# The half routers of a gated-expert kernel spread over other places, with GpSimd waiting for VectorE in all of them

## The chip, the core and the metric

The kernel runs on one core of one Trainium2 chip. The metric is the device time of one execution in microseconds (us). The engines are TensorE (PE, with PEld for its weight loads), VectorE (DVE), ScalarE (ACT), GpSimd (POOL) and SyncE (SP), which issues the DMAs here.

## The reference

The input x is (16, 64, 112, 112): 16 images, 64 channels, 112 x 112 pixels. Cut to what matters:

```python
x = x + scale(_ln_c(x))          # max and mean over the channels, a 3x3 convolution, a sigmoid as a gate
t = _to_tokens(x)                # each pixel is a token of 64 channels
n = _ln_t(t)
router_probs = softmax(n @ router_w + router_b)          # 8 experts
top_p, top_i = top_k(router_probs, 2)
top_p = top_p / sum(top_p)
expert_out = einsum('bnd,edc->bnec', n, expert_w) + expert_b
t = t + einsum('bnk,bnkc->bnc', top_p, take_along_axis(expert_out, top_i))
```

For each token the router needs the largest and the second largest of 8 logits, each as a one-hot row in which only the first of tied logits counts, and two gates that are sigmoids of the gap between the two.

## The kernel before

**Rounds, steps and places.** The images are handled as 8 pairs. The program is one sequence of rounds; in round r three stages run interleaved, each for another pair: A (pair r: loading, centring by matmul, statistics), B (pair r-1: norms, convolution and router, on all pixels of the pair at once) and C (pair r-2: the expert matmuls and the output). Rounds 2 to 7 hold all three; round 0 is A alone, round 1 A and B, round 8 B and C, rounds 9 and 10 C alone. A round has 14 steps of 8 image rows, and each step has two halves on VectorE. So a round has 28 places: place 2s is the first half of step s, place 2s+1 the second.

**Stage C.** Per step TensorE spreads gates over channels into the PSUM tile gb (line 514). VectorE multiplies gb with the pixels xd into gx for six units (line 714); for two more, ScalarE copies gb to gs (line 1003) and GpSimd multiplies (line 1205). TensorE then adds up the experts (line 568) in moe, and VectorE adds moe to tt into the output tile ot (line 727). gb has two slots, so a spread matmul waits for the VectorE product that frees its slot. GpSimd also does the parts subtraction (line 1211, first half of a step) and tt (line 1222, second half).

**Stage B on VectorE** is put into places by `gate`: before the first unit of a half step, the place's operations are issued. Places 1, 2, 3 and 7, 8, 9 hold the two reciprocal roots (`root_guess`, `square_times_e` with line 799 and 801, `third_order`, `second_order`), place 6 `affine`, and place 9 ends with `scale`, which writes rho. Places 12 to 19 hold the router of the first half of the pixels, places 20 to 27 that of the second half: top (line 733, a reduction), ge (736, a comparison), key (741) and key_max (733), oh1 (749) and dl (751), top2 (733) and gap (760), ge2 (736), key2 (741) and key_max2 (733), oh2 (766). The names are the program's order lists; lines 741 and 733 serve both keys. Between key_max and oh1, and between key_max2 and oh2, ScalarE widens the key to 8 columns (`widen`, line 1046); after gap it makes the two gates (`gates`, lines 1052 and 1053). The operations of line 736, 741, 749, 751, 760, 766, 799 and those like them read two SBUF tensors; the reductions read one.

**Stage B on GpSimd** (`router` and `router_tail`): at step 0 `root_of` 1 makes e (line 1295) for the root of place 1; at step 1 `to_pool` (lines 1307, 1309, after tt) makes the convolution's input; at step 3 `affine_of_mean` and `root_of` 2, for place 7; at steps 5 to 7 the scaled and biased logits (lines 1244, 1252); at step 9 `first_gates` (1259) of half 0, at 10 `second_gates` (1265), at 11 `summed_gates` (1274), at 12 `scaled_gates` (1280), at 13 `first_gates` of half 1. `router_tail` does the other three of half 1 in steps 0, 1 and 2 of the next round, ahead of `router`.

**Order between the two engines.** `vector_place` makes GpSimd wait, before its gx of a place, until VectorE has ended that place's operations. In rounds 1 to 7 it does this in places 1, 2, 3, 6, 7, 8, 9 and 26; in round 8 also in places 12 to 27.

The convolution is in TensorE's order in step 2 (`convolve`, line 592), between the spread matmuls of place 5's half and the experts.

Of the kernel before, what the change touches and what calls it, by code (L numbers as in the profile page):

```python
# [52 lines left out]
LAG = 2  # L53
# [25 lines left out]
B_ACT = ("sig", "wide_0", "g1_0", "g2_0", "qa_0", "wide2_0", "wide_1", "g1_1", "g2_1", "wide2_1", "qa_1")  # L79
# [56 lines left out]
def gated_expert_program(nc, x, conv_w, conv_b, router_w, router_b, expert_w, expert_b, const_f, const_g, out):  # L136
# [3 lines left out]
    with ExitStack() as ctx:  # L140
# [57 lines left out]
        rho = sb("rho", [W, 2 * H])  # L198
# [48 lines left out]
        b_dve = sem("b_dve")  # L247
        b_pool = sem("b_pool")
# [48 lines left out]
        b_sem = {B_DVE: b_dve, B_NORM: b_norm, B_POOL: b_pool, B_ACT: b_act}  # L297
# [376 lines left out]
        def _(dve):  # L674
# [63 lines left out]
            def largest_key(r, h, again, rows):  # L738

                own(r, f"ge{again}_{h}")  # L740
                dve.tensor_tensor(key[:, rows, :], ge[:, rows, :], prios, ALU.mult).then_inc(b_dve, 1)
                own(r, f"key{again}_{h}")
                largest(key_max, key, rows).then_inc(b_dve, 1)

            def first_expert(r, h):

                rows = (first, second)[h]
# [6 lines left out]
            def second_logit(r, h):  # L754

                rows = (first, second)[h]
# [5 lines left out]
            def second_expert(r, h):  # L762

                rows = (first, second)[h]
# [643 lines left out]
```

## Time and profile before

| what | value |
|---|---|
| median of 3 runs | 1400.77 us (1400.72 to 1402.35) |
| the profiled execution | 1400.0 us, span of its instructions 1398.1 us |
| TensorE busy | 1291.5 us, 92% of the span |
| VectorE busy | 1243.4 us, 89% |
| GpSimd busy | 1065.5 us, 76% |
| ScalarE busy | 1051.3 us, 75% |
| mean granted TensorE clock | 0.968 |

Busy shares are averages over rounds of different kinds. The wait that ends last in a place is to be looked for in that place: who waits, and for whom. In a timeline, a bracket behind an instruction gives how long its engine had been idle and what released it. An instruction that is held after it was issued shows as a longer one.

### The profile page before, as it was taken

The page shows a single profiled execution, that of the slowest core. Times are in us where ns is not written, and L with a number is a line of the kernel's source. Part 1 is how long each engine was busy: PE and PEld are TensorE (multiplying, and loading weights), DVE is VectorE, ACT ScalarE, POOL GpSimd, SP SyncE. Part 2 cuts the span into 40 slices and gives each one's busy share as a digit, 9 for nine tenths or more (in the row PEclk, how much of TensorE's full clock was granted, in tenths as well). Part 3 has the DMA queues.
Part 4 walks back from the last instruction along what each step waited for, and adds up shares of the span by engine and source line. Part 5 has one row for each costly group of instructions (what it writes and reads, how often), then busy time and mean ns, then how long its engine had stood idle before and what let it go on. Part 6 is the DMA issues. An engine that isn't in the chain of part 4 may idle for free.

```text
span 1398.1 us, 33104 instructions
## 1 busy us (share of the span) xinstructions
PE 1291.5 (92%) x11750; PEld 610.9 (44%) x11750; DVE 1243.4 (89%) x1527; ACT 1051.3 (75%) x3950; POOL 1065.5 (76%) x643
## 2 busy tenths in 40 slices
PE   8854999999999999999999999999999898889998
PEld 8854444444444444444444444444444332223332
DVE  6787799978999899998999889998999889998887
ACT  6677898888988889888898889888988443444442
POOL 6333787887887787887878787887878777789885
PEclk9955999999999999999999999999999998999999
DMA  6442466666666666576676566676665554557774
GB/s 224 124 129 78 145 199 199 198 199 199 199 186 215 195 205 204 176 225 193 204 209 197 189 212 197 193 218 188 207 207 171 152 170 143 164 165 206 204 205 144
DMA packets 85845, 259.97 MB, mean 186 GB/s; under 512 B 13744, under 2 KB 13744, under 8 KB 85680
## 3 DMA queue, kind: packets, MB, share of 16 engines
q1 hardware_dynamic: 85680, 257.85, 61.3%
q8 instruction: 94, 1.54, 0.5%
q14 instruction: 71, 0.58, 0.1%
HBM read 206.42 MB, written 51.38 MB: 184 GB/s over the span
## 4 chain that ended last, share of the span: by engine, by line
PE 56%; DVE 22%; issue 9%; POOL 2%; ACT 2%; DVEq 0%; POOLq 0%; ACTq 0%
PE moe L568 34%; DVE gx L714 12%; PE tm L493 8%; PE gb L514 8%; PE tm L507 2%; DVE ge L736 2%; DVE stats L691 2%; PE moe L562 2%; PE tm L553 2%; DVE ot L727 1%; PE tm L592 1%; DVE oh L749 1%; DVE u L799 1%; POOL dl L1265 1%; DVE top L733 1%
## 5 line engine op out<-in xcount | busy, mean ns | idle before, releaser
L568 PE MATMUL moe<-gx,wc 128*64 128x448 f32 x3584 | 803.7, 554 | 0.0
L714 DVE TENSOR_TENSOR gx<-gb,xd 128x896 f32<-128x896 f32 x672 | 710.6, 1085 | 82.0 <-PE gb L514 76.8
L1205 POOL TENSOR_TENSOR gx<-gs,xd 128x896 f32<-128x896 f32 x224 | 491.0, 2192 | 233.8 <-ACT gs L1003 170.1
L1003 ACT ACTIVATE gs<-gb 128x896 f32<-128x896 f32 x224 | 205.3, 917 | 187.0 <-PE gb L514 181.7
L965 ACT ACTIVATE sq<-xct 112x64 f32<-112x64 f32 x1400 | 338.4, 246 | 7.5 <-DVE early_s L701 2.1
L568 PEld LDWEIGHTS moe<-gx,wc 128*64 128x64 f32 x3584 | 223.5, 136 | 212.2 <-issue 160.8
L965 ACT ACTIVATION_READ_ACCUMULATOR sq<-xct 112x1 f32 x1400 | 265.6, 190 | 0.0
L1222 POOL TENSOR_TENSOR tt<-xc,a1s 128x896 f32<-128x896 f32 x112 | 235.7, 2104 | 11.5 <-issue 9.8
L514 PE MATMUL gb<-s,cg 32*128 32x448 f16 x1792 | 166.7, 360 | 60.5 <-DVE gx L714 59.1
L514 PEld LDWEIGHTS gb<-s,cg 32*128 32x128 f16 x1792 | 45.3, 91 | 386.3 <-DVE gx L714 357.1
L493 PE MATMUL tm<-rhs,xa 64*112 64x74 f32 x2800 | 184.6, 272 | 10.9 <-ACT early_l L950 5.2
L493 PEld LDWEIGHTS tm<-rhs,xa 64*112 64x112 f32 x2800 | 161.6, 182 | 45.7 <-issue 40.3
L727 DVE TENSOR_TENSOR ot<-moe,tt 128x448 f32<-128x448 f32 x224 | 137.3, 613 | 15.5 <-PE moe L568 15.5
L946 ACT ACTIVATE xct<-tm 112x512 f32<-112x512 f32 x175 | 104.0, 594 | 58.1 <-PE tm L493 58.0
L1010 ACT ACTIVATE a1s<-tm,ones 128x896 f32<-128x896 f32 x112 | 112.7, 1007 | 30.3 <-PE tm L553 30.3
L1211 POOL TENSOR_TENSOR parts<-q,parts 112x448 f16<-112x448 f32 x112 | 116.4, 1040 | 9.4 <-ACT parts L988 9.4
L995 ACT ACTIVATE s<-tm 128x896 f16<-128x896 f16 x112 | 101.6, 907 | 0.0
L691 DVE TENSOR_REDUCE stats<-xct 112x8 f32<-112x512 f32 x128 | 86.6, 677 | 6.9 <-ACT logit_mean L950 6.7
L691 DVE TENSOR_REDUCE early_s<-xct 112x8 f32<-112x512 f32 x96 | 65.0, 678 | 19.7 <-ACT early_l L950 19.0
L562 PE MATMUL moe<-s,bw 128*64 128x448 f16 x448 | 80.8, 355 | 0.0
L507 PEld LDWEIGHTS tm<-cg,parts 112*64 112x64 f16 x1792 | 57.2, 111 | 48.1 <-issue 48.1
L988 ACT ACTIVATE parts<-q 112x576 f16<-112x576 f32 x112 | 75.9, 678 | 0.0
(94 smaller groups left out, 1094.4 us busy)
## 6 DMA issues: line engine op xcount, KB each, us to landing
xd<-in_x_dram SPq DMA_DIRECT2D x448, 224.0 KB, 4.0
xa<-in_x_dram SPq DMA_DIRECT2D x112, 448.0 KB, 4.4
xc<-in_x_dram SPq DMA_DIRECT2D x112, 448.0 KB, 4.8
out_dram<-ot SPq DMA_DIRECT2D x112, 448.0 KB, 3.5
gx<-in_const_g_dram SPq DMA_DIRECT2D x1, 384.0 KB, 5.6
cf<-in_const_f_dram SPq DMA_DIRECT2D x1, 333.5 KB, 3.1
cf<-in_L_ffn_expert_b_dram SPq DMA_DIRECT2D x12, 1.0 KB
gx<-in_L_ffn_expert_w_dram SPq DMA_DIRECT2D x1, 128.0 KB, 5.5
```

Of the source, the lines that this page charges most:

```text
L493: last = pe.matmul(pair[:, b, j, :], xa[chans, step % XA, row * W:(row + 1) * W], rhs1[chans, :], start=True, stop=True)
L514: last = pe.matmul(gb[:, 2 * slot + b, 0:HALF], cg[rows, k * P:(k + 1) * P], s[rows, v % 2, c * HALF:(c + 1) * HALF], start=True, stop=True)
L568: last = pe.matmul(moe[b * CH:(b + 1) * CH, c, 0:HALF], wc[:, k * CH:(k + 1) * CH], gx[:, u, b, :], start=False, stop=(k == KT - 1), skip_ ...
L691: dve.tensor_reduce(to[:, 0, lo + cols.start:lo + cols.stop], xct[:, step % 2, cols, :], AX.X, ALU.max) \
L714: dve.tensor_tensor(gx[:, i, :, :], gb[:, 2 * slot:2 * slot + 2, 0:HALF], xd[:, v % 2, :, c * HALF:(c + 1) * HALF], ALU.mult).then_inc(sca ...
L727: dve.tensor_tensor(ot[:, sl, cols], moe[:, c, 0:HALF], tt[:, sl, cols], ALU.add).then_inc(final, 1)
L965: last = act.activation(sq[:, n, :], xct[:, step % 2, n, :], ACT.Square, accum_out=to[:, 1, lo + n:lo + n + 1])
L1003: act.activation(gs[:, j, :, :], gb[:, 2:4, 0:HALF], ACT.Copy).then_inc(gate_out, 1)
L1010: act.activation(a1s[:, v % 2, :].rearrange("p (c t) -> p c t", c=2), tm[:, :, 0:HALF], ACT.Identity, bias=ones[:, :], scale=1.0).then_inc ...
L1205: pool.tensor_tensor(gx[:, ND + j, :, :], gs[:, j, :, :], xd[:, v % 2, :, j * HALF:(j + 1) * HALF], ALU.mult).then_inc(scaled_p, 1)
L1211: pool.tensor_tensor(quadrants(v)[:, :, :, QN:QUAD], q_blocks(v, AGAIN, BLOCK), high_again(v), ALU.subtract).then_inc(rest1, 1)
L1222: pool.tensor_tensor(tt[:, sl, :], xc[:, sl, :], a1s[:, sl, :], ALU.mult).then_inc(scaled_x, 1)
```

## The change

The 12 operations of a half router on VectorE go into 10 places instead of 8: oh1 and dl part, key2 and key_max2 part. Half 0 takes places 12 to 21 and half 1 starts at 22. Its last three groups come in the next round: ge2 in place 0, key2 and key_max2 together in place 4, oh2 in place 5. They have a semaphore of their own, `b_late`. ScalarE's `gates` of half 0 moves from step 8 to 9, its second `widen` from 9 to 10, half 1's first `widen` from 11 to 12, its `gates` from 12 to step 0 and its second `widen` from 13 to step 2 of the next round. On GpSimd, half 0's `second_gates`, `summed_gates` and `scaled_gates` go from steps 10, 11, 12 to 11, 12, 13; half 1's `first_gates` goes from step 13 to step 0 of the next round, `second_gates` from 0 to 3, `summed_gates` and `scaled_gates` from 1 and 2 both to 4, and `router_tail` now comes after `router`. rho gets two buffers, since the late `scaled_gates` reads it while the next round's is written; `scale` waits for the round before last instead of the last one. `vector_place` waits in all router places in all rounds, the late ones too. In the diff, lines without a change are mostly left out, of the fifth part the removed lines too; a few small hunks (the b_late semaphore, rhos for rho, the group that a wait names) are not shown.

```diff
@@ -70,13 +70,14 @@
+B_LATE = ("ge2_1", "key2_1", "key_max2_1", "oh2_1")
-         + tuple(n + "_1" for n in HALF_ROUTER))
+         + tuple(n + "_1" for n in HALF_ROUTER if n + "_1" not in B_LATE))
-B_ACT = ("sig", "wide_0", "g1_0", "g2_0", "qa_0", "wide2_0", "wide_1", "g1_1", "g2_1", "wide2_1", "qa_1")
+B_ACT = ("sig", "wide_0", "qa_0", "g1_0", "g2_0", "wide2_0", "wide_1", "g1_1", "g2_1", "qa_1", "wide2_1")
@@ -313,19 +315,20 @@
-        PLACE_END = {1: "t_a1", 2: "y_a1", 3: "r1", 6: "v2", 7: "t_a2", 8: "y_a2", 9: "rho",
-                     26: "key_max2_1"}
-        TAIL_END = {1: "t_a1", 2: "y_a1", 3: "r1", 6: "v2", 7: "t_a2", 8: "y_a2", 9: "rho"}
-        HALF_END = ("top", "ge", "key_max", "dl", "d", "ge2", "key_max2", "oh2")
-        for place in range(16):
-            TAIL_END[12 + place] = f"{HALF_END[place % 8]}_{place // 8}"
+        ROOT_END = {1: "t_a1", 2: "y_a1", 3: "r1", 6: "v2", 7: "t_a2", 8: "y_a2", 9: "rho"}
+        HALF_END = {12: "top_0", 13: "ge_0", 14: "key_max_0", 15: "oh1_0", 16: "dl_0", 17: "d_0", 18: "ge2_0",
+                    19: "key2_0", 20: "key_max2_0", 21: "oh2_0", 22: "top_1", 23: "ge_1", 24: "key_max_1",
+                    25: "oh1_1", 26: "dl_1", 27: "d_1"}
+        LATE_END = {0: "ge2_1", 4: "key_max2_1", 5: "oh2_1"}
-            ends = TAIL_END if r == PAIRS else PLACE_END
-            if 1 <= r <= PAIRS and place in ends:
-                b_done(eng, r, B_DVE, ends[place])
+            if r <= PAIRS and place in ROOT_END:
+                b_done(eng, r, B_DVE, ROOT_END[place])
+            if r <= PAIRS and place in HALF_END:
+                b_done(eng, r, B_DVE, HALF_END[place])
+            if 2 <= r <= PAIRS + 1 and place in LATE_END:
+                b_done(eng, r - 1, B_LATE, LATE_END[place])
@@ -735,35 +738,53 @@
+            def tie_key(r, h, rows):
+                own(r, f"ge_{h}")
+            def first_of_ties(r, h, rows):
+                own(r, f"key_{h}")
+            def second_tie_key(r, h, rows, group):
+                b_done(dve, r, group, f"ge2_{h}")
+                dve.tensor_tensor(key[:, rows, :], ge[:, rows, :], prios, ALU.mult).then_inc(b_sem[group], 1)
+            def second_of_ties(r, h, rows, group):
+                b_done(dve, r, group, f"key2_{h}")
+                largest(key_max, key, rows).then_inc(b_sem[group], 1)
+            def first_expert(r, h, rows):
+            def logits_left(r, h, rows):
+            def second_logit(r, h, rows):
+            def second_at_top(r, h, rows, group):
+                own(r, f"top2_{h}")
+                at_top(dl, top2, rows).then_inc(b_sem[group], 1)
+            def second_expert(r, h, rows, group):
+                dve.tensor_tensor(oh2[:, rows, :], prios, ge[:, rows, :], ALU.is_equal).then_inc(b_sem[group], 1)
@@ -775,18 +796,32 @@
                 elif place == 2:
-                    largest_key(r, h, "", rows)
+                    tie_key(r, h, rows)
+                    first_of_ties(r, h, rows)
                 elif place == 3:
-                    first_expert(r, h)
+                    first_expert(r, h, rows)
                 elif place == 4:
-                    second_logit(r, h)
+                    logits_left(r, h, rows)
                 elif place == 5:
-                    own(r, f"top2_{h}")
-                    at_top(dl, top2, rows).then_inc(b_dve, 1)
+                    second_logit(r, h, rows)
                 elif place == 6:
-                    largest_key(r, h, "2", rows)
+                    second_at_top(r, h, rows, B_DVE)
+                elif place == 7:
+                    second_tie_key(r, h, rows, B_DVE)
+                elif place == 8:
+                    second_of_ties(r, h, rows, B_DVE)
                 else:
-                    second_expert(r, h)
+                    second_expert(r, h, rows, B_DVE)
+            def late_router(r, place):
+                if place == 0:
+                    second_at_top(r, 1, second, B_LATE)
+                elif place == 4:
+                    second_tie_key(r, 1, second, B_LATE)
+                    second_of_ties(r, 1, second, B_LATE)
+                elif place == 5:
+                    second_expert(r, 1, second, B_LATE)
@@ -834,9 +869,9 @@
-                if due(count := b_at(r, len(B_POOL), 0)):
+                if due(count := b_at(r - 1, len(B_POOL), 0)):
-                dve.scalar_tensor_tensor(out=rho[:, :], in0=av, scalar=1.0, in1=r2[:, :],
+                dve.scalar_tensor_tensor(out=rhos[:, r % 2, :], in0=av, scalar=1.0, in1=r2[:, :],
@@ -859,10 +894,10 @@
                     scale(r)
-                elif 12 <= place < 20:
+                elif 12 <= place < 22:
                     half_router(r, 0, place - 12)
-                elif place >= 20:
-                    half_router(r, 1, place - 20)
+                elif place >= 22:
+                    half_router(r, 1, place - 22)
...
@@ -899,6 +936,8 @@
+                    if tail:
+                        late_router(r - 1, 2 * step + 1)
                     if Bp:
...
@@ -1056,15 +1095,18 @@
                     widen(r, 0, "")
-                elif step == 8:
+                elif step == 9:
                     gates(r, 0)
-                elif step == 9:
+                elif step == 10:
                     widen(r, 0, "2")
-                elif step == 11:
+                elif step == 12:
                     widen(r, 1, "")
-                elif step == 12:
+            def late_router(r, step):
+                if step == 0:
                     gates(r, 1)
-                elif step == 13:
+                elif step == 2:
                     widen(r, 1, "2")
@@ -1104,6 +1146,8 @@
                         turned_to_sbuf(r, v + 1)
+                    if tail:
+                        late_router(r - 1, step)
                     if Bp:
...
@@ -1331,22 +1375,21 @@
                     first_gates(r, 0)
-                elif step == 10:
+                elif step == 11:
                     second_gates(r, 0)
-                elif step == 11:
+                elif step == 12:
                     summed_gates(r, 0)
-                elif step == 12:
+                elif step == 13:
                     scaled_gates(r, 0)
-                elif step == 13:
+            def router_tail(r, step):
+                if step == 0:
                     first_gates(r, 1)
-            def router_tail(r, step):
-                if step == 0:
+                elif step == 3:
                     second_gates(r, 1)
-                elif step == 1:
+                elif step == 4:
                     summed_gates(r, 1)
-                elif step == 2:
                     scaled_gates(r, 1)
@@ -1364,10 +1407,10 @@
                         rest_one(r, v + 2)
+                    if Bp:
+                        router(r, step)
                     if tail:
                         router_tail(r - 1, step)
-                    if Bp:
-                        router(r, step)
                     if ahead:
                         scale_unit(r, v + 1, 0)
```

## Rows read from the trace of the kernel before

**Rows 1.** The page, part 1: busy us, share of the span, instructions.
```profile
PE 1291.5 (92%) x11750; PEld 610.9 (44%) x11750; DVE 1243.4 (89%) x1527; ACT 1051.3 (75%) x3950; POOL 1065.5 (76%) x643
```

**Rows 2.** The chain that ended last, line 592: start us, us, what.
```profile
794.50 2.46 PE tm L592 x12
956.07 2.46 PE tm L592 x12
```

**Rows 3.** Timeline of TensorE, round 6: start us, us, engine, line, op.
```profile
832.18 0.37 PE L514 MATMUL gb<-s,cg 32*128 32x448 f16 x4
...
837.64 0.37 PE L514 MATMUL gb<-s,cg 32*128 32x448 f16 x4
...
849.40 0.37 PE L514 MATMUL gb<-s,cg 32*128 32x448 f16 x4 [0.36 <-DVE gx L714]
```

**Rows 4.** Timeline of VectorE, round 6, places 14 and 15.
```profile
846.61 0.62 DVE L741 TENSOR_TENSOR key<-ge,prio 112x896 bf16<-112x896 bf16 x1
847.26 1.09 DVE L733 TENSOR_REDUCE key_max<-key 112x112 bf16<-112x896 bf16 x1
...
852.41 1.22 DVE L749 TENSOR_TENSOR oh<-prio,ge 112x896 bf16<-112x896 bf16 x1
853.66 1.09 DVE L751 SCALAR_TENSOR_TENSOR dl<-oh,lg 112x896 f32<-112x896 bf16 x1
```

**Rows 5.** Timeline of VectorE, round 6, places 24 and 25.
```profile
905.42 0.28 DVE L760 TENSOR_TENSOR gap<-top 112x112 f32<-112x112 f32 x1
...
909.75 1.67 DVE L736 TENSOR_TENSOR ge<-dl,top 112x896 bf16<-112x896 f32 x1
```

**Rows 6.** Timeline of GpSimd, round 6, place 14.
```profile
851.03 2.12 POOL L1252 TENSOR_TENSOR lg<-lg,brb 112x896 f32<-112x896 f32 x1
```

**Rows 7.** Timeline of VectorE, round 8, places 13 and 15.
```profile
1159.93 5.18 DVE L736 TENSOR_TENSOR ge<-lg,top 112x896 bf16<-112x896 f32 x1
...
1176.60 2.86 DVE L751 SCALAR_TENSOR_TENSOR dl<-oh,lg 112x896 f32<-112x896 bf16 x1
```

**Rows 8.** Timeline of GpSimd, round 8, the same stretch.
```profile
1162.38 1.78 POOL L1244 TENSOR_TENSOR lg<-logit_mean,rho 112x896 f32<-112x896 f32 x1
...
1176.03 2.48 POOL L1252 TENSOR_TENSOR lg<-lg,brb 112x896 f32<-112x896 f32 x1
```

**Rows 9.** Timeline of GpSimd, round 6, places 0 to 9.
```profile
769.52 1.75 POOL L1265 TENSOR_TENSOR dl<-oh,g 112x896 f32<-112x896 bf16 x1
...
781.50 2.09 POOL L1274 TENSOR_TENSOR q<-lg,dl 112x896 f32<-112x896 f32 x1
...
788.89 0.78 POOL L1307 TENSOR_TENSOR pooled<-stats,r 112x224 f32<-112x224 f32 x1
...
793.56 1.79 POOL L1280 TENSOR_TENSOR q<-q,rho 112x896 f32<-112x896 f32 x1
...
816.62 1.03 POOL L1211 TENSOR_TENSOR parts<-q,parts 112x448 f16<-112x448 f32 x1
820.30 2.15 POOL L1205 TENSOR_TENSOR gx<-gs,xd 128x896 f32<-128x896 f32 x1 [2.65 <-DVE rho L839]
```

**Rows 10.** Timeline of VectorE, round 6, places 1, 3, 7 and 9.
```profile
771.82 0.28 DVE L794 TENSOR_SCALAR p<-e 112x224 int32<-112x224 int32 x1 [1.19 <-POOL e L1295]
...
782.45 1.39 DVE L799 TENSOR_TENSOR u<-p 112x224 f32<-112x224 f32 x1
...
807.94 0.28 DVE L794 TENSOR_SCALAR p<-e 112x224 int32<-112x224 int32 x1 [0.32 <-POOL e L1295]
...
818.57 0.38 DVE L799 TENSOR_TENSOR u<-p 112x224 f32<-112x224 f32 x1
```

**Rows 11.** Windows: us, busy us by engine, granted clock, DMA share, GB/s.
```profile
82.10:128.20 46.10, 22.90 (x224) 21.49 (x224) 40.27 (x52) 31.55 (x120) 13.40 (x9) 0.50 0.42 120
...
1155.40:1249.40 94.00, 75.52 (x562) 25.53 (x560) 90.99 (x86) 37.44 (x49) 72.74 (x40) 0.93 0.54 157
1279.40:1288.30 8.90, 8.90 (x76) 3.16 (x78) 7.42 (x8) 4.11 (x5) 7.91 (x5) 1.00 0.75 208
```

More of the change, by code:

```diff
@@ L197, in gated_expert_program @@
         gap = sb("gap", [W, 2 * H])
-        rho = sb("rho", [W, 2 * H])
+        rhos = sb("rhos", [W, 2, 2 * H])
         top = sb("top", [W, 2 * H])
@@ L247, in gated_expert_program @@
         b_dve = sem("b_dve")
+        b_late = sem("b_late")
         b_pool = sem("b_pool")
@@ L752, in first_expert @@
                                          op0=ALU.mult, op1=ALU.add).then_inc(b_dve, 1)
-            def second_logit(r, h):
-                rows = (first, second)[h]
+            def second_logit(r, h, rows):
                 own(r, f"dl_{h}")
@@ L760, in second_logit @@
                 dve.tensor_tensor(gap[:, rows], top2[:, rows], top[:, rows], ALU.subtract).then_inc(b_dve, 1)
-            def second_expert(r, h):
-                rows = (first, second)[h]
+            def second_at_top(r, h, rows, group):
+                own(r, f"top2_{h}")
+                at_top(dl, top2, rows).then_inc(b_sem[group], 1)
+            def second_expert(r, h, rows, group):
                 b_done(dve, r, B_ACT, f"wide2_{h}")
-                dve.tensor_tensor(oh2[:, rows, :], prios, ge[:, rows, :], ALU.is_equal).then_inc(b_dve, 1)
+                dve.tensor_tensor(oh2[:, rows, :], prios, ge[:, rows, :], ALU.is_equal).then_inc(b_sem[group], 1)
             def half_router(r, h, place):
@@ L882, in early_body, with body @@
                         gate(r, step, True)
-            def body(r, A, Bp, steps=STEPS):
+            def body(r, A, Bp, steps=STEPS, tail=True):
                 for step in range(steps):
@@ L887, in body @@
                     cur, ahead = on(r, v), on(r, v + 1)
+                    if tail:
+                        late_router(r - 1, 2 * step)
                     if Bp:
@@ L921, in _ @@
             body(PAIRS + 1, False, False)
-            body(PAIRS + 2, False, False, LAG + 1)
+            body(PAIRS + 2, False, False, LAG + 1, False)
         @block.scalar
@@ L1044, in widen @@
                 rows = (first, second)[h]
-                b_done(act, r, B_DVE, f"key_max{again}_{h}")
+                b_done(act, r, B_LATE if again and h == 1 else B_DVE, f"key_max{again}_{h}")
                 act.activation(ge[:, rows, :], wide(key_max, rows), ACT.Copy).then_inc(b_act, 1)
@@ L1106, in body @@
                         turned_to_sbuf(r, v + 1)
+                    if tail:
+                        late_router(r - 1, step)
                     if Bp:
@@ L1245, in logits_scaled @@
                                    logit_mean[:, h * H // 2:(h + 1) * H // 2, :, 0:E],
-                                   rho[:, rows].rearrange("w (h b) -> w h b", b=2).unsqueeze(3)
+                                   rhos[:, r % 2, rows].rearrange("w (h b) -> w h b", b=2).unsqueeze(3)
                                    .to_broadcast([W, H // 2, 2, E]), ALU.mult).then_inc(b_pool, 1)
@@ L1278, in scaled_gates @@
                 own(r, f"qb_{h}")
-                rhos = rho[:, rows].unsqueeze(2).unsqueeze(3).to_broadcast([W, H, 2, B_LO])
+                rho = rhos[:, r % 2, rows].unsqueeze(2).unsqueeze(3).to_broadcast([W, H, 2, B_LO])
                 pool.tensor_tensor(q_tokens[:, rows, QG:QG + E].rearrange("w n (i e) -> w n i e", i=2),
-                                   bias_cols(rows), rhos, ALU.mult).then_inc(b_pool, 1)
+                                   bias_cols(rows), rho, ALU.mult).then_inc(b_pool, 1)
             def root_of(r, n, of):
@@ L1333, in router @@
                     first_gates(r, 0)
-                elif step == 10:
+                elif step == 11:
                     second_gates(r, 0)
-                elif step == 11:
+                elif step == 12:
                     summed_gates(r, 0)
-                elif step == 12:
+                elif step == 13:
                     scaled_gates(r, 0)
-                elif step == 13:
-                    first_gates(r, 1)
             def router_tail(r, step):
                 if step == 0:
+                    first_gates(r, 1)
+                elif step == 3:
                     second_gates(r, 1)
-                elif step == 1:
+                elif step == 4:
                     summed_gates(r, 1)
-                elif step == 2:
                     scaled_gates(r, 1)
```

9 lines of the change are left out of this document (2 added, 7 removed).

## The prediction

> **What bounds the kernel now.** I read the page's first part, then TensorE's timeline, then VectorE's and GpSimd's side by side. TensorE is busy 92% of the span and VectorE 89% [rows 1], so the question is which of them sets each half step. The chain that ended last passes the convolution once a round, at 794.50 and 956.07: a full round is 161.57 us, or 28 half steps (places) [rows 2].
>
> TensorE's spread matmuls (line 514) pace the places. From 832.18 to 837.64 (place 12) is 5.46 us without a wait; the next two places take 11.76 us, to 849.40, which waits 0.36 on VectorE's gx of line 714 [rows 3]. So TensorE's floor is about 5.45. Of the 11.76 us, 5.86 are place 14's, where VectorE put 0.62 + 1.09 us of router work, some 1.66 once neighbours overlap by a few hundredths, ahead of gx [rows 4]. I use **T = max(5.45, 4.15 + g)**, with g the router or root work in a place, contention included. Up to 1.30 us is free; all above it reaches the end. Place 5 alone has the 2.46 us of convolution on top [rows 2] and a VectorE that waits there.
>
> Part of g is no work. In place 15 the one-hot op at 852.41 takes 1.22 us and ends 0.5 after GpSimd's line 1252 has ended (851.03 + 2.12) [rows 4, 6]. In round 8 the comparison at 1159.93 takes 5.18 us: it sits through the end of a gx, the parts subtract and line 1244 (1162.38 + 1.78), and ends 0.95 after that [rows 7, 8]. GpSimd's ops followed each other without a gap and none let VectorE in. But at 1176.60 the dl op, issued 0.04 us after the one before it ended, is held for 2.86 by a line 1252 that had been waiting since 1176.03 (2.48 instead of 2.12) [rows 6 to 8]. So a VectorE op with two SBUF inputs and a GpSimd op exclude each other, a waiting GpSimd op slips between two VectorE ops, and reductions (1.09, [rows 4]) don't suffer.
>
> **The change, router places 12 to 27 of rounds 2 to 7.** The same ops are issued; only their places change.
> - Places 15 and 23 held oh1 and dl together: 1.22 + 1.09, less the overlap, is g 2.25, T 6.40. Now oh1 alone and dl a place later. GpSimd's waits at places 14 and 24 start its gx at 848.35 instead of 847.95 (key_max's end, [rows 4, 6]), so line 1252 ends 0.4 later and oh1 takes 1.6, g 1.55, T 5.70. dl (1.09) is below 1.30. Saved: 0.7 a pair, 1.4.
> - Of four key plus key_max pairs (T 5.83 each) two stay (14, 24), one is split into two free places, one goes to place 4 of the next round. Saved here: 2 x 0.37 = 0.7.
> - The second comparison of half 1 took 1.67 us at 909.75, behind a GpSimd op [rows 5]. It moves to the next place 0, empty until now. There GpSimd's tt ends just as it begins, so 1.1, free. Saved 0.3.
> - top2 (a reduction like key_max, 1.09) and gap, 0.28 [rows 4, 5], stay together at 1.30: free, no slack left. ACT's widening and its two sigmoids move with them; they follow places already ended.
>
> Sum -2.4 a round, six rounds: **-14.5**.
>
> **Its head, places 0 to 9.** GpSimd's tail (first_gates 1.73 like its sister op of 1.75 at line 1265, second_gates 1.75, summed_gates 2.09, scaled_gates 1.79 [rows 9]) moves from steps 13, 0, 1, 2 to steps 0, 3, 4, 4.
> - Place 1: VectorE waited 1.19 us for GpSimd's e, which stood behind line 1265 [rows 9, 10]. Now e goes first, at 769.5. But first_gates follows at once, to 771.8, and VectorE's second root op (two inputs) must wait for its end. It ends at 772.05 instead of 772.52 (771.82 + 0.28 and 0.42 for u): -0.5.
> - Place 3: u took 1.39 instead of 0.38, behind summed_gates (781.50 + 2.09) [rows 9, 10]. That op is gone from here: g 1.2, T 5.45 for 6.29: -0.8.
> - Place 4, empty before, gets key2 and key_max2: 0.62 + 1.09. Since place 3 shrinks, key2 comes as GpSimd's tt ends; the two pooled ops follow without a gap (788.89 + 0.78 [rows 9]; the second taken as long). No hold gives T 5.8, one 6.5, both 7.3. I take 6.65: +1.2.
> - Place 5: oh2 falls into the convolution: 0.
> - Place 7: after e, second_gates now starts; VectorE's p needs 0.28 (807.94), its u is then held until 809.6. u ended at 808.64 before (807.94 + 0.28 + 0.42), now at 809.9 [rows 10]: +1.25.
> - Place 9: parts ends at 817.65 and GpSimd then idles 2.65 us, until rho [rows 9]. VectorE's four root ops started at 818.57 undisturbed (u 0.38 [rows 10]). Now summed_gates fills 817.65 to 819.75 and scaled_gates follows. u waits 1.1 us; scaled_gates, waiting, slips in before the second op as line 1252 did, another 1.75 us, less what was free. T becomes 8.2 instead of 5.72: +2.5. If scaled_gates goes ahead of u too, 8.5; if VectorE kept its turn through all four ops, 6.7.
>
> Places 4, 7 and 9 cost 4.95 in each of rounds 2 to 7, 29.7; places 1 and 3 give 1.3 in rounds 3 to 7, 6.5. Together **+23.2**. GpSimd's later gx and tt cost nothing: TensorE reads a gx some 6 us after it is made at place 9, and it idled 2.65 us there [rows 9].
>
> **Round 8 and 9.** GpSimd already waits in every place of round 8, so only the layout counts. VectorE is busy 91.0 of 94.0 us in places 12 to 27 and TensorE 75.5 [rows 11]; any unblocked time is gained. Splitting 15 and 23 stops cases like dl's 2.86, but dl now meets a tt, ending in the same 1-2 us hold. Walking the 16 places with the lock as above gives 89.6 for 96.6: -7. The head by the same terms: place 1 -0.4, place 3 -1.8, place 4 +0.7, place 7 +1.2, place 9 +3.4 (two holds, floor 4.45): +3.1. Round 9 runs at TensorE's floor, 8.90 busy of 8.90 [rows 11]; places 0 and 4 rise above its half of 4.45: +1.9. Sum **-2.0**. The granted clock there was 0.93 [rows 11], for which I put nothing.
>
> **Round 1** has no expert work. Between 82.1 and 128.2 VectorE is busy 40.3 of 46.1 us [rows 11]. Four ops leave it (ge2 some 2.0 with its hold, 0.61, 1.09, 0.6), 4.1 us net of overlap; one ScalarE wait on key_max fewer gives up to 1 more; the two sigmoids in front of round 2 take 0.6. **-4.4**, between -1 and -6.
>
> **Sum.** -14.5 + 23.2 - 2.0 - 4.4 = +2.3 us on the profiled execution's 1400.0 (span 1398.1), so 1402.3. The median of the runs stands 0.8 above it: **1403**.
>
> The Trainium skill ("SBUF — State Buffer", Who interferes with whom) says that the first to issue holds the shared pair for its whole instruction and the other blocks fully. On the hold this case's rows agree. On the order they don't: at 1159.93 VectorE asked first, and two later GpSimd ops went ahead [rows 7, 8].
>
> **Rivals.**
> 1. *GpSimd wins at every seam*, as at 1159.93. Place 4 is held by both pooled ops (7.3) and place 9 at 8.5: +0.7 and +0.3 in six rounds, 1409. For it speaks that seam; against it 1176.
> 2. *VectorE keeps its turn* (the other sign). Place 9 costs 6.7 and place 4 5.8: 1.5 and 0.85 less in six rounds, 14 less, 1389. Place 9 decides: faster than before once its hold is under some 2.0 us a round. Against it speaks 1176.60.
> 3. *First come, first served at each seam.* key2 is then held by one op at most, the comparison of place 13 in round 8 by one: 0.6 x 6 and some 1.7 less, 1398. The Trainium skill's rule above is this rival.
> 4. *The waits of GpSimd become the cost.* Its 0.4 us delay at places 14 and 24 is handed on to dl, ge and oh1: 0.2 at four places in six rounds, 1408. Against it, GpSimd is busy only 76% of the span [rows 1].
> 5. *It does nothing*: what one place gives, a neighbour takes: 1401.
>
> **How the numbers follow.** A measurement of this kernel can tell 0.2%, 2.8 us, from no change. Forecast 0.45 (own range 1399 to 1407: same 0.25, slower 0.18, faster 0.02); rival 1 0.18, slower; rival 2 0.14, faster; rival 3 0.12, faster 0.08 and same 0.04; rival 4 0.06, slower; rival 5 0.05, same. Faster 0.24, same 0.34, slower 0.42. The range leaves out the far half of rival 2 and the top of rival 1: 1390 to 1411, which takes in place 4's 5.8 to 7.3, place 9's 6.7 to 8.5 and round 1's -1 to -6.
>
> **What would show it.** Convolution to convolution in the middle rounds about 162.8 instead of 161.57. VectorE's first root u at place 9 about 1.5 us and the op after it 2 us (scaled_gates at 1.75 between them), and GpSimd's wait on rho gone or shorter than 2.65. The place 3 root op back at 0.39; at place 7 u about 1.6. No 2.25 us pair of oh1 and dl. Round 1 shorter by 4 us. I am wrong if the root ops of place 9 run undisturbed, if key at place 4 takes 0.6 or over 1.5, or if spread matmuls wait on something other than line 714.

## The result and the profile after

The changed kernel takes **1419.8 us** (median of 4 runs, 1417.4 to 1420.3), the kernel before 1400.7: a ratio of 1.0132, 95% interval 1.0118 to 1.0147. The forecast was 1403, within 1390 to 1411: 17 us short, with the result outside the range.

The page of the changed kernel, busy time and the clock by slices:
```profile
span 1418.5 us, 33160 instructions
...
PE 1309.3 (92%) x11750; PEld 618.1 (44%) x11750; DVE 1270.3 (90%) x1527; ACT 1051.5 (74%) x3950; POOL 1049.4 (74%) x643
...
PEclk9955999999999999998999989999899999999999
```
Against [rows 1] TensorE issues the same 11750 matmuls and is busy 17.8 us longer. A wait would not show in busy time, so the matmuls themselves are slower. VectorE's 26.9 us more for the same 1527 instructions are ops held longer. The clock's row, in slices of 35 us, hides this almost wholly.

The chain that ended last, the convolution (now line 595), against [rows 2]:
```profile
144.37 2.46 PE tm L595 x12
...
306.94 2.46 PE tm L595 x12
...
471.27 2.45 PE tm L595 x12
...
636.98 2.46 PE tm L595 x12
...
804.21 2.46 PE tm L595 x12
...
971.41 2.46 PE tm L595 x12
```
Before, a round takes 161.57. Now they take 162.57, 164.33, 165.71, 167.23 and 167.20. No work differs between these rounds, so a cost that is not in the layout comes on top.

TensorE's timeline in round 6, places 7 to 11:
```profile
821.28 0.37 PE L517 MATMUL gb<-s,cg 32*128 32x448 f16 x4 [1.50 <-DVE gx L717]
821.58 1.01 PE L496 MATMUL tm<-rhs,xa 64*112 64x74 f32 x16
822.52 3.06 PE L571 MATMUL moe<-gx,wc 128*64 128x448 f32 x8
...
829.55 1.72 PE L571 MATMUL moe<-gx,wc 128*64 128x448 f32 x8
...
836.34 0.53 PE L517 MATMUL gb<-s,cg 32*128 32x448 f16 x4 [2.54 <-DVE gx L717]
836.80 1.78 PE L496 MATMUL tm<-rhs,xa 64*112 64x74 f32 x16
838.50 3.25 PE L571 MATMUL moe<-gx,wc 128*64 128x448 f32 x8
...
846.17 1.72 PE L571 MATMUL moe<-gx,wc 128*64 128x448 f32 x8
```
Windows behind the pause of place 9, in round 6 and in round 2 (us, busy us of PE, PEld, DVE, ACT and POOL with their instructions, granted clock, DMA share, GB/s):
```profile
829.50:836.00 6.50, 4.30 (x30) 1.42 (x26) 6.40 (x8) 4.66 (x20) 5.24 (x4) 1.00 0.51 157
836.00:843.00 7.00, 6.66 (x36) 2.86 (x38) 4.30 (x6) 2.47 (x11) 3.48 (x2) 0.53 0.52 131
843.00:850.00 7.00, 7.00 (x72) 3.23 (x68) 5.32 (x7) 5.88 (x23) 6.60 (x4) 0.98 0.60 201
...
176.00:182.00 6.00, 6.00 (x66) 2.92 (x66) 4.87 (x7) 5.14 (x22) 4.83 (x4) 1.00 0.70 177
```
TensorE waits 2.54 us for VectorE, and then the same eight expert matmuls take 3.25 us instead of 1.72. The granted clock is 0.53 for 7 us, that is almost wholly the lower level of 1.2 GHz. Place 10, which holds no router or root work, takes 8.59 us (836.34 to 844.93) where it took 5.44. In round 2 the pause is as long (2.56) and the clock stays at 1.00. From round 3 to 7 place 10 takes 7.06, 8.58, 8.57, 8.59, 8.59, and place 8, behind the 1.50 us pause, takes 7.03 in rounds 5 to 7. Against 5.44 these eight places lose 19.0 us. **That is the miss:** the rest of the change comes to +1.4 on the span, where I had +2.3.

VectorE at places 1, 4, 7, 9, 15, 16 of round 6, against [rows 4, 5, 10]:
```profile
780.90 1.36 DVE L829 TENSOR_SCALAR p<-e 112x224 int32<-112x224 int32 x1
...
798.07 0.70 DVE L754 TENSOR_TENSOR key<-ge,prio 112x896 bf16<-112x896 bf16 x1
...
817.58 1.79 DVE L829 TENSOR_SCALAR p<-e 112x224 int32<-112x224 int32 x1 [0.24 <-POOL e L1339]
819.41 0.39 DVE L834 TENSOR_TENSOR u<-p 112x224 f32<-112x224 f32 x1
...
831.32 1.25 DVE L834 TENSOR_TENSOR u<-p 112x224 f32<-112x224 f32 x1
832.60 1.82 DVE L836 SCALAR_TENSOR_TENSOR u<-u,e 112x224 f32<-112x224 f32 x1
...
870.57 1.63 DVE L764 TENSOR_TENSOR oh<-prio,ge 112x896 bf16<-112x896 bf16 x1
...
876.26 1.12 DVE L769 SCALAR_TENSOR_TENSOR dl<-oh,lg 112x896 f32<-112x896 bf16 x1
```
GpSimd beside them, against [rows 6, 9]:
```profile
798.24 1.16 POOL L1351 TENSOR_TENSOR pooled<-stats,r 112x224 f32<-112x224 f32 x1
...
817.51 1.73 POOL L1309 TENSOR_TENSOR dl<-oh,g 112x896 f32<-112x896 bf16 x1
...
830.23 2.09 POOL L1318 TENSOR_TENSOR q<-lg,dl 112x896 f32<-112x896 f32 x1
832.40 1.78 POOL L1324 TENSOR_TENSOR q<-q,rhos 112x896 f32<-112x896 f32 x1
835.36 2.08 POOL L1249 TENSOR_TENSOR gx<-gs,xd 128x896 f32<-128x896 f32 x1 [1.18 <-DVE rhos L874]
```
Each of GpSimd's ops can be laid over the VectorE op that it holds. Line 834 starts at 831.32 under the q of line 1318 and ends 0.25 after it. Line 836 starts at 832.60, 0.20 after the next q, and ends 0.24 after that. With first_gates at place 1 and second_gates at place 7, four GpSimd ops of 1.7 to 2.1 us each thus meet four VectorE ops whose own time is 0.3 to 0.4 us.

Rounds 8 and 9, places 12 to 27 and two late places, against [rows 11]:
```profile
1181.60:1266.80 85.20, 72.24 (x578) 25.39 (x576) 84.84 (x85) 36.76 (x47) 73.76 (x41) 1.00 0.61 174
1277.70:1286.60 8.90, 8.90 (x74) 3.17 (x72) 7.41 (x9) 4.11 (x5) 7.21 (x5) 1.00 0.71 205
```

### The profile page after: what moved, and what is told of

It is laid out like the page before. It is cut to its first block, busy times and chain, and to the rows that moved or that the text cites. A ratio compares the mean times of both kernels' runs of the same rounds, so it can differ in the third digit from the quotient of the medians.

```text
span 1418.5 us, 33160 instructions
## 1 busy us (share of the span) xinstructions
PE 1309.3 (92%) x11750; PEld 618.1 (44%) x11750; DVE 1270.3 (90%) x1527; ACT 1051.5 (74%) x3950; POOL 1049.4 (74%) x643
## 4 chain that ended last, share of the span: by engine, by line
PE 62%; DVE 19%; issue 8%; POOL 2%; ACT 1%; DVEq 0%; POOLq 0%; ACTq 0%
PE moe L571 38%; DVE gx L717 10%; PE tm L496 9%; PE gb L517 8%; PE tm L510 2%; PE moe L565 2%; PE tm L556 2%; DVE p L829 1%; DVE stats L694 1%; DVE ge L739 1%; PE tm L595 1%; DVE oh L764 1%; DVE u L836 1%; DVE u L834 1%; DVE ot L730 1%
## 5 line engine op out<-in xcount | busy, mean ns | idle before, releaser
L571 PE MATMUL moe<-gx,wc 128*64 128x448 f32 x3584 | 816.5, 562 | 0.0
L1249 POOL TENSOR_TENSOR gx<-gs,xd 128x896 f32<-128x896 f32 x224 | 468.9, 2093 | 275.8 <-ACT gs L1042 181.3
L496 PE MATMUL tm<-rhs,xa 64*112 64x74 f32 x2800 | 189.0, 277 | 10.6 <-ACT logit_mean L989 5.4
L496 PEld LDWEIGHTS tm<-rhs,xa 64*112 64x112 f32 x2800 | 165.8, 186 | 46.2 <-issue 42.8
L985 ACT ACTIVATE xct<-tm 112x512 f32<-112x512 f32 x175 | 104.1, 595 | 72.3 <-PE tm L496 72.2
```

Of the source, the lines that this page charges most:

```text
L496: last = pe.matmul(pair[:, b, j, :], xa[chans, step % XA, row * W:(row + 1) * W], rhs1[chans, :], start=True, stop=True)
L571: last = pe.matmul(moe[b * CH:(b + 1) * CH, c, 0:HALF], wc[:, k * CH:(k + 1) * CH], gx[:, u, b, :], start=False, stop=(k == KT - 1), skip_ ...
L1249: pool.tensor_tensor(gx[:, ND + j, :, :], gs[:, j, :, :], xd[:, v % 2, :, j * HALF:(j + 1) * HALF], ALU.mult).then_inc(scaled_p, 1)
```

## The experiments

All ratios are to the kernel before on the same chip. "Half clock" is the time lost in rounds 2 to 7 by places behind a pause (their length less 5.44), counted like the 19.0 above. That column and the places are read from the one profiled execution of each kernel. Executions of one kernel differ: those of e8 take 1423.7 to 1431.9 us, at mean clocks of 0.963 to 0.955, so a few us of that column would come out otherwise in another execution.

| kernel | GpSimd's late router ops | VectorE's router places | waits in rounds 1 to 7 | us | places 7 / 9 | half clock |
|---|---|---|---|---|---|---|
| before | old | old | few | 1400.7 | 5.6 / 5.7 | 0 |
| after | as changed | spread | all | 1419.8 | 7.0 / 8.1 | 19.0 |
| e1 | as changed | spread | none | 1410.2 | 7.0 / 8.1 | 9.5 |
| e8 | as changed | old | few | 1428.9 | 7.0 / 8.1 | 18.4 |
| e2 | sums later | spread | all | 1393.4 | 7.0 / 5.7 | 0 |
| e3 | second earlier | spread | all | 1400.2 | 5.5 / 8.1 | 7.8 |
| e4 | cleared | spread | all | 1371.7 | 5.5 / 5.7 | 0 |
| e7 | cleared | spread | none | 1365.5 | 5.5 / 5.7 | 0 |
| e9 | cleared | old | few | 1426.6 | 5.5 / 5.7 | 14.4 |
| e11 | cleared | old | all | 1399.1 | 5.5 / 5.7 | 6.4 |
| e12 | old | old | all | 1414.0 | 5.6 / 5.7 | 4.8 |
| e5, e10 | old; a VectorE op more at place 9 | old | few | 1424.7, 1402.9 | 5.5 / 8.05, 6.86 | 10.9, 0 |
| e6 | old; a VectorE op more at places 7 and 9 | old | few | 1425.0 | 6.6 / 8.1 | 4.8 |

**e1, the new waits taken out again** (the waits at the root places stay):
```diff
-            if r <= PAIRS and place in HALF_END:
+            if r == PAIRS and place in HALF_END:
                 b_done(eng, r, B_DVE, HALF_END[place])
-            if 2 <= r <= PAIRS + 1 and place in LATE_END:
-                b_done(eng, r - 1, B_LATE, LATE_END[place])
```


> The changed kernel, but GpSimd waits for VectorE in the router places only in round 8, as before the change; the late places have no wait either. Theory (holds by GpSimd's moved tail ops at places 7 and 9, and the clock that falls behind them): the waits matter little, 1417 to 1421 us, places 7 and 9 still 7.0 and 8.1 us, the granted clock still at half for 3.4 to 6.8 us a round from round 3 on. Rival (the added waits push GpSimd back and that is the loss): 1408 or less, places 7 and 9 shorter.

Measured 1410.2 (ratio 1.0067, 1.0052 to 1.0082), below what I expected and above the rival's 1408, whose shorter places 7 and 9 did not come either. Places 15 and 25 fall from 5.70 to 5.42, about 0.6 us a round, 4 in all. Places 7 and 9 pause as long as in the changed kernel (1.50, 2.59), but the clock falls less often behind them: 9.5 us are lost instead of 19.0. The stretch from round 8's place 5 to round 9's gives 2.9 back. So the kernel is faster without the waits, and most of the difference came by way of the clock. Why pauses of the same length bring fewer falls here is not shown, so only the direct 4 us can be put down to the waits themselves.

**e2, e3, e4: GpSimd's late ops away from VectorE's root ops.** e2 moves the two sums behind tt:
```diff
-                elif step == 4:
+
+            def router_last(r, step):
+
+                if step == 4:
                     summed_gates(r, 1)
+                elif step == 5:
                     scaled_gates(r, 1)
...
                         scale_x(r, v + 1)
+                    if tail:
+                        router_last(r - 1, step)
```
e3 moves `second_gates` from step 3 to between gx and tt of step 2:
```diff
-                elif step == 3:
-                    second_gates(r, 1)
...
                         scale_unit(r, v + 1, 0)
+                    if tail and step == 2:
+                        second_gates(r - 1, 1)
```
e4 does both, and `first_gates` goes from step 0 to step 2.

> The changed kernel, but summed_gates of half 1 is issued in step 4 after tt (behind place 9's root ops) and scaled_gates in step 5 after tt. Theory: place 9 falls from 8.1 to 5.7 us (2.4 in six rounds, 3.4 in round 8), place 7 stays at 7.0, place 13 rises by up to 0.6 because GpSimd's logits come later; without TensorE's 2.5 us pause at place 9 the granted clock no longer falls in the middle rounds, another 15 to 19 us: 1383 to 1392 us. If the clock falls by place 7's 1.5 us pause alone: 1395 to 1405. Rival (the ops only hold up VectorE somewhere else, the total of holds stays): above 1410.

> The changed kernel, but second_gates of half 1 is issued in step 2 between GpSimd's gx and tt (behind the convolution, where VectorE has no work) instead of in step 3. Theory: place 7 falls from 7.0 to 5.6 us (1.45 in seven rounds, 10 us), place 9 stays at 8.1 with its 2.5 us pause; if that pause alone makes the clock fall, some 10 to 15 us of clock loss stay: 1400 to 1410 us. If the fall needs both pauses close together: 1388 to 1395. Rival (holds only move): above 1415.

> The changed kernel with all four GpSimd tail ops out of the way of root ops: first_gates in step 2 before place 5's gx, second_gates in step 2 between gx and tt, summed_gates in step 4 after tt, scaled_gates in step 5 after tt. Theory: places 1, 7, 9 at 5.45, 5.6, 5.7 us (0.9, 1.45, 2.4 less), place 13 up to 0.6 more, no fall of the clock in rounds 2 to 7: 1370 to 1380 us, below the kernel before. Rival (spreading the router itself costs, or holds only move): 1400 or above.

Measured 1393.4 (0.9946, 0.9931 to 0.9961), 1400.2 (0.9996, 0.9986 to 1.0007) and **1371.7** (0.9790, 0.9776 to 0.9805). In e2 the 2.5 us pause is gone and no place behind a pause in rounds 2 to 7 is lengthened by the clock, though the 1.50 us pause of place 7 stays. It ends 1.4 us above the range I gave for that case: places 13 to 15 take 0.9 us more a round, since GpSimd's logits come later, and I had put 0.6. In e3 the 2.5 us pause stays, and four rounds of six still lose 1.6 to 3.0 us behind it. In e4 round 6 reads, on VectorE:
```profile
803.75 0.38 DVE L835 TENSOR_TENSOR u<-p 112x224 f32<-112x224 f32 x1
804.17 0.39 DVE L837 SCALAR_TENSOR_TENSOR u<-u,e 112x224 f32<-112x224 f32 x1
```
and on GpSimd:
```profile
801.75 1.03 POOL L1259 TENSOR_TENSOR parts<-q,parts 112x448 f16<-112x448 f32 x1
805.49 2.09 POOL L1253 TENSOR_TENSOR gx<-gs,xd 128x896 f32<-128x896 f32 x1 [2.71 <-DVE rhos L877]
807.54 2.09 POOL L1270 TENSOR_TENSOR tt<-xc,a1s 128x896 f32<-128x896 f32 x1
809.60 2.10 POOL L1322 TENSOR_TENSOR q<-lg,dl 112x896 f32<-112x896 f32 x1
```
GpSimd idles 2.71 us while the root ops run free, and the same q starts 5.9 us behind the first u instead of 1.1 ahead of it, beside places 10 and 11, which hold no router or root work. A round is 158.8 us. The whole loss hung on where four GpSimd ops stand, and with them out of the way the kernel is 29 us faster than before. Not all of that is the spreading: places 1 and 3 fall to 5.46 each, where the kernel before was held too (6.46 and 6.30), some 9 us in rounds 3 to 7.

**e5, e6, e10: the pause without the change.** The kernel before, with one VectorE reduction more ahead of the root ops of place 9, from round 2 on (its result is not used):
```diff
+                pads[0] += 1
+                src = cf[0:W, CC:CC + length].unsqueeze(1).to_broadcast([W, n, length])
+                dve.tensor_reduce(pad_out[:, 0:n], src, AX.X, ALU.max).then_inc(padded, 1)
...
+                    pad(r, 7, 312)
                     second_order(r, 2, r2)
```
It takes 2.42 us in e5, 1.23 in e10; e6 has the one of e5 and one of 1.47 at place 7.

> The kernel before the change, with one more VectorE operation at place 9 from round 2 on: a reduction of constants into a scratch tile, sized for 2.4 us, which no GpSimd operation can hold. Place 9 should take 8.1 us as in the changed kernel, 16.8 us in seven rounds: 1417.7 us if the granted clock stays. If a TensorE pause of 2.5 us is what makes the clock fall, whatever causes it, up to 15 us more and half-clock stretches behind place 9: up to 1433. Rival (the fall needs GpSimd's holds or the spread router): no fall, 1416 to 1419.

> As the one-pad kernel, and a reduction sized for 1.45 us at place 7 too, so both places take what they take in the changed kernel (7.0 and 8.1 us) on the layout of before. 27 us in seven rounds: 1428 us if the clock stays; with falls as in the changed kernel (19 us) 1438 to 1448. Rival (pauses don't make the clock fall): 1426 to 1430.

> The kernel before the change with a reduction of 1.2 us at place 9 from round 2 on, half of the larger pad. Place 9 takes 6.9 us, TensorE pauses 1.3 us: 8.4 us in seven rounds, 1409.3 us with no half-clock stretch in rounds 2 to 7, if the clock falls only behind the longer pauses of 2.5 us. Rival (any added pause at this place brings falls): 1414 or more, with half-clock stretches behind place 9.

Measured 1424.7 (1.0164, 1.0142 to 1.0186), 1425.0 (1.0170, 1.0153 to 1.0186) and 1402.9 (1.0016, 1.0007 to 1.0026). Windows of e5 in round 6, before and behind the end of its pause:
```profile
836.00:838.00 2.00, 0.00 (x0) 0.00 (x0) 1.93 (x4) 0.81 (x8) 0.71 (x1) 0.95 0.00 0
838.00:845.00 7.00, 6.73 (x36) 2.97 (x38) 4.27 (x6) 2.50 (x11) 3.42 (x2) 0.53 0.50 129
845.00:852.00 7.00, 7.00 (x70) 3.05 (x66) 5.29 (x7) 6.16 (x23) 6.63 (x4) 1.00 0.60 199
```
With no GpSimd op moved, the pause of 2.52 us and the clock behind it are the changed kernel's: place 10 takes 7.04, 8.59, 7.06, 5.44, 8.34 and 7.05 in rounds 2 to 7. So a pause of this length is enough, whichever of the two ways it is made. In e6 the pad of place 7 lay partly over a wait, so that the pause there was 1.03 us, and nothing followed it; it tells nothing of a 1.5 us pause. Its total is 13 us under the 1438 to 1448 that I expected and a little under the rival's 1426 to 1430 (pauses don't make the clock fall), but the trace does not bear that rival out: three rounds still fall behind the 2.5 us pause of place 9, 4.8 us in all against 10.9 in e5.

e10 halves the op: the pause is 1.33 us, place 9 takes 6.86, and no round falls. The sum came out 6 us below what I expected: a round is only 0.85 us longer, and the stretch from round 8's place 5 to round 9's is 3.6 shorter. Places 13 and 14 of round 8 give as much by themselves, with 5.83 and 6.25 us instead of 8.65 and 7.03; the rest of that stretch cancels. The comparison held there for 5.18 us in [rows 7] is held 2.37 in e10:
```profile
1169.06 2.37 DVE L738 TENSOR_TENSOR ge<-lg,top 112x896 bf16<-112x896 f32 x1
```
```profile
1168.39 2.09 POOL L1220 TENSOR_TENSOR gx<-gs,xd 128x896 f32<-128x896 f32 x1
1170.43 1.88 POOL L1226 TENSOR_TENSOR parts<-q,parts 112x448 f16<-112x448 f32 x1
```
GpSimd has the same ops in the same order there, and VectorE asks 0.67 us after the gx has started, against 0.59 before. This time it gets in behind the gx, and parts is the one that stretches. In all kernels of the table but the one before and e12, place 13 of round 8 takes 5.6 to 5.8 us; so in every other comparison with the kernel before, some 3.6 us may be this hold and not what the row names.

**e8, GpSimd's late ops alone** moved as in the change, in the kernel before (with the two buffers of rho, and `router_tail` behind `router`):
```diff
-                elif step == 13:
+
+            def router_tail(r, step):
+
+                if step == 0:
                     first_gates(r, 1)
-
-            def router_tail(r, step):
-
-                if step == 0:
+                elif step == 3:
                     second_gates(r, 1)
-                elif step == 1:
+                elif step == 4:
                     summed_gates(r, 1)
-                elif step == 2:
                     scaled_gates(r, 1)
```


> The kernel before the change with only GpSimd's tail of half 1 moved as in the change (first_gates to step 0 of the next round, second_gates to 3, summed_gates and scaled_gates to 4, router ahead of tail, two buffers of rho); VectorE's and ScalarE's router as before. Theory: places 7 and 9 rise by 1.45 and 2.4 us, place 3 falls by 0.8, place 1 by 0.15: 2.9 us in rounds 3 to 7, 3.9 in round 2, some 3 in round 8, so 1422 us, and with a falling clock 1425 to 1442. Rival (the loss is in the router's spreading, or in the added waits): 1405 or less.

Measured 1428.9 (1.0184, 1.0152 to 1.0217): 28 us more than before, 9 more than the whole change. Places 7 and 9 take 7.03 and 8.12 as there, and place 10 takes 8.4 to 8.6 in all six rounds. The spreading of VectorE's router therefore gains: e8 to e1 adds it and no waits in the middle rounds, and gives 18.7 us, of which 8.9 are fewer falls of the clock.

**e7, e9, e11, e12: spreading and waits, each with and without the other.** e7 is e4 with the waits of e1 taken out and half 1's `logits_biased` one step later. e9 is the kernel before with e4's placing of the late ops. e11 is e9, and e12 the kernel before, with the round 8 waits in every round:
```diff
-            ends = TAIL_END if r == PAIRS else PLACE_END
+            ends = TAIL_END
```


> The kernel with the cleared tail (1371.7 us), with GpSimd's waits in the router places in round 8 alone, and half 1's biased logits in step 8 instead of 7, where VectorE has dl and a reduction. Theory (a place costs what its held operations cost above 1.3 us): place 15 from 6.4 to 5.45 us, place 25 from 5.7 to 5.45, place 14 from 6.26 to 6.0: 1.5 us in six rounds, 1361 to 1365 us, no fall of the clock. Rival (the waits keep more holds away than they cause): 1370 or above.

> The kernel before the change with the cleared GpSimd tail (first_gates of half 1 in step 2, second_gates in step 2 between gx and tt, summed_gates in step 4 after tt, scaled_gates in step 5 after tt), VectorE's and ScalarE's router and GpSimd's waits as before. Places 1 and 3 fall by 1.0 and 0.8 us, places 13 to 15 rise by up to 1 together: 1390 to 1396 us. If the spreading of the router is worth what the places say (2.4 us a round, 4 in round 1), this stays 18 us or more above the kernel that has both, 1371.7. Rival (the cleared tail is all of the gain, spreading gives nothing): 1376 or less.

> This is e9 (router as before, tail of GpSimd cleared from VectorE's root places) with the one thing that e9 lacks beside e4's GpSimd: GpSimd waits for VectorE in every router place of every round. My theory of e9's loss is that oh1 at place 15 was overtaken by four GpSimd ops because nothing made GpSimd stop for it. Then with the waits oh1 is held by one op at most, about 2.3 us as in e2 and e4, dl adds 1.0, place 15 takes about 7.5 us instead of 11.59, TensorE's pause there is about 2.0 instead of 6.1, and place 16 falls from 7.8 to 5.45: some 6.4 us a round less over six rounds, 38 us: 1388 us, up to 1396 if the 2.0 us pause brings the half clock in some rounds or if place 23 pays 0.4 more. The rival, that the cleared tail and the old router collide whatever GpSimd waits for, says that oh1 is still held by more than 4 us, and at least 1410 us.

> The kernel before with one part of the change alone: GpSimd waits for VectorE in every router place of every round, with the old placing of router and tail. By e1, where taking the waits out shortened places 15 and 25 by 0.27 us each, putting them in costs here about 0.3 us at places 15 and 23, where oh1 and dl stand together: 0.6 us a round in six rounds, some 4 us: 1404 us (1401 to 1408), with no half clock in rounds 2 to 7, since no pause grows past 1.3 us. The rival, that GpSimd has slack and takes the delay up, says 1401 us. A second rival, that the waits also remove holds in the router as they do in e4 beside e9, says under 1398 us.

Measured: e7 **1365.5** (0.9744, 0.9728 to 0.9759), the fastest kernel here; e9 1426.6 (1.0189, 1.0172 to 1.0206); e11 1399.1 (0.9990, 0.9981 to 0.9999); e12 1414.0 (1.0092, 1.0079 to 1.0106).

e9 was the worst miss. Its roots are as clear as e4's, but place 15 takes 11.59 us in every middle round. VectorE and GpSimd there, in round 6 of e9:
```profile
875.86 6.40 DVE L750 TENSOR_TENSOR oh<-prio,ge 112x896 bf16<-112x896 bf16 x1
```
```profile
874.64 1.02 POOL L1215 TENSOR_TENSOR parts<-q,parts 112x448 f16<-112x448 f32 x1
875.64 2.08 POOL L1256 TENSOR_TENSOR lg<-lg,brb 112x896 f32<-112x896 f32 x1
877.68 2.06 POOL L1209 TENSOR_TENSOR gx<-gs,xd 128x896 f32<-128x896 f32 x1
879.71 2.06 POOL L1226 TENSOR_TENSOR tt<-xc,a1s 128x896 f32<-128x896 f32 x1
```
oh has been issued at 875.86, and two GpSimd ops that start later go ahead of it. GpSimd waits for nothing in between, VectorE gets in after tt at 881.77, TensorE pauses 6.1 us, and the clock falls behind that in all six rounds. e11 puts in the wait and nothing else, the same place:
```profile
856.15 2.36 DVE L748 TENSOR_TENSOR oh<-prio,ge 112x896 bf16<-112x896 bf16 x1
858.55 1.09 DVE L750 SCALAR_TENSOR_TENSOR dl<-oh,lg 112x896 f32<-112x896 bf16 x1
```
```profile
855.92 2.11 POOL L1254 TENSOR_TENSOR lg<-lg,brb 112x896 f32<-112x896 f32 x1
859.72 2.08 POOL L1207 TENSOR_TENSOR gx<-gs,xd 128x896 f32<-128x896 f32 x1 [1.69 <-DVE dl L750]
```
GpSimd now waits 1.69 us for dl, oh is held by one op, and place 15 takes 7.54, as expected. The total gained 27.6 us instead of 38: the 2.06 us pause that is left brings the half clock in four of six rounds (6.4 us), place 23 pays 0.5 a round, and the rest lies in small terms. So the waits are worth 28 us in e11 and cost 13 in e12. There was no such hold to prevent in e12; they lengthen places 15 and 23 by 0.5 each, as place 23 in e11, some 1.5 a round in all, and place 24 loses 1.6 in three rounds behind a pause of 1.40. I had priced e12 at 4 us: the direct cost is 9, and the clock's 4.8 I had left out, the same omission once more. With the waits and a cleared GpSimd, spreading alone is worth 27.4 us (e11 to e4), 6.4 of them falls of the clock that e4 does not have.

## Why the prediction was wrong

**The step that failed** is the one that carries the whole sum, "T = max(5.45, 4.15 + g)", taken as the full price of a place. TensorE's pause is about T less 5.45, and the formula ends there. The clock may fall behind a pause, and the next place, here 8 or 10, then costs up to 3.15 us more. I had the pause at place 9 right (+2.5, with T 8.2) and asked nothing about what follows it. The only mention of the clock is in round 8: "The granted clock there was 0.93 [rows 11], for which I put nothing". That row should have been a rival: in the kernel before, rounds 2 to 7 pause for under 1 us at a place and show no fall, and round 8, where VectorE is behind, has them. The range could not hold the result, as none of the five rivals had this term.

The Trainium skill ("TensorE: Matmul & The Clock Gate", The HAM clock gate) names both levels and says that the clock depends on how busy TensorE has been lately, in a window that runs free of the kernel. The trace agrees on the levels (0.53 against 1.00) and that a pause comes first. That its phase is why one round falls and the next doesn't would fit, but no run here shows it.

**Point by point**, measured in rounds 3 to 7 unless said otherwise:

| term | forecast | measured |
|---|---|---|
| places 12 to 27, a round | -2.4 | -2.2 |
| place 1 | -0.5 | -0.15 |
| place 3 | -0.8 | -0.83 |
| place 4 | +1.2 | +0.45 |
| place 5 | 0 | -0.05 |
| place 7 | +1.25 | +1.45 |
| place 9 | +2.5 | +2.34 |
| places 8 and 10, half clock, all rounds | none | +19.0 |
| rounds 8 and 9 | -2.0 | -1.2 |
| up to round 2's convolution | -4.4 | -3.9 |

- **Router places.** 15 and 25 take 5.70 as forecast, 23 takes 5.73 for 6.38. Place 14 takes 6.01, 0.2 above its term. The pair of oh1 and dl is parted (870.57 and 876.26).
- **Place 4.** No hold by the pooled ops to speak of: key takes 0.70, where a sign of my being wrong was 0.6. It started at 798.07, the pooled op at 798.24, and that one was stretched to 1.16 from 0.78. Here the first to come went first, as in rival 3; I chose the middle of a range, and its lower end was right.
- **Places 1 and 7.** "a VectorE op with two SBUF inputs and a GpSimd op exclude each other" is too narrow. The op held is the one before u, p of line 829, a tensor_scalar with one input: 1.36 and 1.79 us for 0.28, and u then ran in 0.39. The sum came out near, since the same GpSimd op holds one or the other. The Trainium skill ("SBUF — State Buffer", Who interferes with whom) does count tensor_scalar among the ops that can take the shared pair; the trace agrees, and I had used only its two-input rule.
- **Place 9.** As forecast to 0.2: 1.25 for u, 1.82 for the next with scaled_gates between them, GpSimd's wait for rho 1.18 instead of 2.65.
- **Rounds 8 and 9.** Right in sum by luck: places 12 to 27 gave 11.3, not 7 (96.6 to 85.2), places 0 to 11 cost 7.1, not 3.1, and round 9 paid 3.1 at its places 0 and 4, not 1.9. Of the 11.3, 3.6 are places 13 and 14, where the comparison is held 2.36 us instead of 5.18; e10 has the same gain on the old places, so it does not take the spreading to make it. The clock moved too: it was 1.00 in places 12 to 27 against 0.93 before, and TensorE was busy 72.2 us there for the same 578 matmuls instead of 77.9; in places 0 to 11 it was 0.93 against 0.97, and TensorE was busy 62.2 instead of 59.1.
- **Round 1.** The -3.9 is near the forecast by luck as well. Place 5 of round 2 starts 5.5 us earlier than before (139.03 against 144.49), and 1.6 of that are lost in the place itself, since the clock has not yet risen: 0.60 in the 4 us ahead of the convolution, where it was 1.00 before.
- **Rivals.** 1 and 2 are out by place 4 and place 9. 3 holds at place 4 and at place 9 too (line 836 asked 0.2 after line 1324), which is what my own term says there; it fails in e9, as at 1159.93 in [rows 7]. 4 is half right: without the waits the kernel is 9.6 us faster (e1), of which 4 are direct and were in my terms for places 15 and 25. 5 is out by the measured time and by e8.

**Shown:** the loss comes from GpSimd's late ops beside VectorE's root ops (e2 to e4, e8), by way of pauses of TensorE, which bring falls of the clock also when made another way (e5). Of the span's 20.4 us more, 19.0 are the clock in rounds 2 to 7; without the new waits the loss is half as large (e1), at pauses of the same length. **Open:** why an equal pause brings a fall in one round and not in the next, so that the number of falls can't be forecast from the layout, only bounded (0 to 3.15 us a pause); and when GpSimd's next op passes a waiting VectorE op (e9, and round 8's place 13 before) and when not (place 4, and that place 13 in e10).

## What to carry to other kernels

Price a pause of TensorE at its own length plus what the clock may take behind it; here 2.5 us of pause cost up to 5.7. Before moving a GpSimd op, lay it over VectorE's short ops in the same place: two of them, 3.9 us together, beside four 0.4 us ops cost 2.4 us a round and the clock behind it; moved behind those ops they cost 0.9, by what they delayed (e2). A wait of GpSimd for VectorE was a cost where no long hold was there to prevent (e12), and worth its price where GpSimd would have run several ops ahead of a waiting VectorE op (e11 against e9).

## What the runs showed of the hardware

- TensorE's granted clock in rounds 2 to 7, by the pause of TensorE in the place before, over the profiled executions of this study: none of 6 rounds fell behind 1.03 us; 7 of 48 behind 1.33 to 1.51; 4 of 6 behind 2.06; 27 of 36 behind 2.5 to 2.65; 6 of 6 behind 6.1. A fall cost 1.6 or 2.3 to 3.15 us in one place.
- A VectorE tensor_scalar of int32 with a single input was held for 1.79 us (0.28 free) by a GpSimd tensor_tensor (the changed kernel, place 7).
- A VectorE op was held for 6.40 us, its own time 0.6, while three GpSimd ops ended, two of which had started after it (e9). With one wait of GpSimd for VectorE it was held 2.36 (e11).
- The same comparison, issued 0.59 us after the start of a GpSimd op and followed by the same GpSimd ops, took 5.18 us in the kernel before; issued 0.67 after it, it took 2.37 (e10).
